# Keys turned by the DMA instead of by the matrix engine, with two small jobs moved between engines

## The reference, cut to what matters

```python
xn = _layernorm(x, ln1_w, ln1_b)               # x: the context, 16 x 1601 x 128
ln = _layernorm(latents, ln2_w, ln2_b)         # 16 x 64 x 128
q = ln @ Wq
kv = jnp.concatenate([xn, ln], axis=-2) @ Wkv
k, v = jnp.split(kv, 2, axis=-1)               # heads: 16 x 64
logits = jnp.einsum('bhld,bhsd->bhls', q * scale, k * scale)
w = jax.nn.softmax(logits, axis=-1)
out = jnp.einsum('bhls,bhsd->bhld', w, v)
return out.reshape(B, L, INNER) @ Wo
```

## Time and profile before

| | |
|---|---|
| median of 3 runs | 2209.73 us |
| the profiled execution | 2206.32 us, span 2204.6 us |
| PE busy | 2042.9 us (93%) |
| DVE busy | 1704.4 us (77%) |
| ACT busy | 1370.1 us (62%) |
| POOL busy | 566.5 us (26%) |
| first cross attention | from 7 us to 932 us |
| second cross attention | from 1168 us to 2041 us |
| DMA in all | 95.18 MB, mean 43 GB/s |

### The profile page before, as it was taken

One profiled execution on the slowest core, in us unless ns is written; L12 is line 12 of the kernel. 1 busy time (PEld: TensorE's weight loads), 2 busy tenths in 40 slices (PEclk: granted clock), 3 DMA queues, 4 the chain that ended last, 5 costly groups with the idle time before them and its releaser, 6 DMA issues. The chain is left out here.

```text
span 2204.6 us, 38627 instructions
## 1 busy us (share of the span) xinstructions
PE 2042.9 (93%) x11914; PEld 1118.3 (51%) x11914; DVE 1704.4 (77%) x4268; ACT 1370.1 (62%) x2468; POOL 566.5 (26%) x584
## 2 busy tenths in 40 slices
PE   7899999999999999889798999999999999999786
PEld 5454545454545455533566444454545454544584
DVE  7789797988888887589667777777786868685557
ACT  3377676766666676644323587868687878777211
POOL 4433333333333332059101102121111111110000
PEclk9899999999999999989999899999999999999897
DMA  2211111111010100033103011111111011100100
GB/s 80 78 48 48 48 48 47 47 47 54 40 63 31 63 31 32 9 93 124 47 1 109 5 36 55 52 35 36 35 36 35 36 35 36 35 32 1 28 1 10
DMA packets 40903, 95.18 MB, mean 43 GB/s; under 512 B 11436, under 2 KB 26776, under 8 KB 40760
## 3 DMA queue, kind: packets, MB, share of 16 engines
q1 hardware_dynamic: 40760, 93.61, 12.3%
HBM read 65.15 MB, written 27.92 MB: 42 GB/s over the span
## 5 line engine op out<-in xcount | busy, mean ns | idle before, releaser
L1122 DVE TENSOR_TENSOR x_p_lo<-x_psum,x_p_hi 128x512 f16<-128x512 f32 (+2 forms) x896 | 606.4, 683 | 195.4 <-ACT x_psum L913 159.5
L912 ACT ACTIVATE x_p_hi<-x_psum 128x512 f16<-128x512 f32 (+2 forms) x480 | 287.9, 600 | 267.8 <-PE x_psum L750 266.0
L912 ACT ACTIVATE x_p_hi<-x_psum,x_bcol 128x512 f16<-128x512 f32 (+1 forms) x416 | 292.3, 703 | 104.2 <-PE x_psum L750 102.3
L770 PE MATMUL x_psum<-x_p_hi,x_x_both 128*128 128x512 f16 (+1 forms) x832 | 316.8, 381 | 42.3 <-DVE x_p_lo L1122 42.1
L748 PE MATMUL x_psum<-x_q,x_xT_both 128*128 128x512 f16 x832 | 316.6, 381 | 0.2
L772 PE MATMUL x_psum<-x_p_hi,x_x_both 128*128 128x512 f16 (+1 forms) x832 | 315.8, 380 | 0.0
L771 PE MATMUL x_psum<-x_p_lo,x_x_both 128*128 128x512 f16 (+1 forms) x832 | 315.8, 380 | 0.0
L750 PE MATMUL x_psum<-x_q,x_xT_both 128*128 128x512 f16 x832 | 315.6, 379 | 0.0
L749 PE MATMUL x_psum<-x_q,x_xT_both 128*128 128x512 f16 x832 | 315.6, 379 | 0.0
L913 ACT ACTIVATE x_psum<-x_psum 128x512 f32<-128x512 f32 (+2 forms) x480 | 287.3, 598 | 0.6
L825 PE MATMUL x_psum<-x_xT_both,x_q 128*128 128x512 f16 (+2 forms) x1024 | 268.3, 340 | 18.4 <-DVE x_mx L1068 6.4
(11 more groups left out here) (450 smaller groups left out, 3404.6 us busy)
## 6 DMA issues: line engine op xcount, KB each, us to landing
context_rows<-x_x_both SPq DMA_DIRECT2D x16, 832.0 KB, 3.5
context_cols<-x_xT_both SPq DMA_DIRECT2D x16, 832.0 KB, 4.9
x_xT_both<-context_cols SPq DMA_DIRECT2D x16, 832.0 KB, 4.5
x_x_both<-context_rows SPq DMA_DIRECT2D x16, 832.0 KB, 6.3
x_raw<-in_ctx SPq DMA_DIRECT2D x16, 768.0 KB
ssm_c_row<-ssm_bc_rows SPq DMA_DIRECT2D x16, 512.0 KB, 4.3
ssm_b_wide<-ssm_bc_rows SPq DMA_DIRECT2D x7, 512.0 KB
x_mrow<-in_mask_BxS_bk SPq DMA_DIRECT2D x16, 200.1 KB
```

Of the source, the lines that this page charges most:

```text
L770: pe.matmul(out, v_hi, p_hi[r][rows, :], start=start, stop=False)
L912: act.activation(p_hi[r][rows, :], score[r][rows, :], ACT.Exp, scale=SCORE_UNIT, **bias).then_inc(p_hi_ready, 1)
L1122: v.tensor_tensor(p_lo[r][rows, :], score[r][rows, :], p_hi[r][rows, :], ALU.subtract).then_inc(p_lo_ready, 1)
```

## The change

In words:

- The first layer's `x` items are gone from PE, ACT and DVE. POOL splits `xt` right after it has normalized it, into a new buffer `x16` (`halves`). SP stores `x16` to `context_rows`, waits until the store has landed, and loads `xT_both` back from there by transposing DMAs in three parts: `front` (hi, tiles 0 to 6), `back` (hi, tiles 7 to 12) and `low` (lo, all 13 tiles), then `x_both` by a plain DMA.
- The second layer loads `xT_both` in the same three parts from `context_rows`; `context_cols` is gone.
- `max` items come in another order: the eight that need only `front` first, then the eight that need `back`. They begin in unit 2 of a first body (before: 4 in the first layer, 3 in the second) and in unit 6 of a second one.
- The latents' sums are copied by DVE instead of ACT, and `later_high` goes from ACT to POOL.
- Mean and variance of the 13 tiles come from five instructions on 13 columns instead of 13 bn_aggr.
- The mask's row and column forms are made at two different places. The last three pairs are handled as: loop of pairs 1 to 5, pairs 6 and 7 unrolled.
- In the folding part POOL normalizes and splits context 0, and SP stores it and issues its loads before the block ends.

```diff
-NORM_STEPS = 2 * KT + 1 + RSQRT_STEPS
+NORM_STEPS = KT + 5 + 1 + RSQRT_STEPS
...
+        def turned_part(sp, n, par, s, j, k):
+            rows = kept_rows[bass.ds(n, 1), :, s:s + 1, j:k, :].rearrange("o p s j d -> (o p) (s j d)")
+            out = xT_both[par][:, s, j * P:k * P].rearrange("p (j k) -> p j k", k=P)
+            return sp.dma_start(out, rows, transpose=True)
+        def load_xT_front(sp, n, par):
+            turned_part(sp, n, par, 0, 0, FRONT).then_inc(xT_front[par], 16)
+        def load_xT_rest(sp, n, par):
+            turned_part(sp, n, par, 0, FRONT, KT).then_inc(xT_back[par], 16)
+            turned_part(sp, n, par, 1, 0, KT).then_inc(xT_low[par], 16)
+        def store_x(sp, n):
+            wait_alone(sp, x16_ready, n + 1)
+            sp.dma_start(kept(n), x16[:, :, :, :]).then_inc(x_stored, 16)
+            wait_alone(sp, x_stored, 16 * (n + 1))
...
+        def halves(pool, n):
+            if not (isinstance(n, int) and n == 0):
+                wait_alone(pool, x_stored, 16 * n)
+            wait_alone(pool, xt_ready, n + 1)
+            pool.tensor_copy(x16[:, 0, :, :], xt[:, :, :]).then_inc(x_hi_ready, 1)
+            wait_alone(pool, x_hi_ready, n + 1)
+            pool.tensor_tensor(x16[:, 1, :, :], xt[:, :, :], x16[:, 0, :, :], ALU.subtract).then_inc(x16_ready, 1)
...
-                for j in range(KT):
-                    steps.mark(v.bn_aggr(xmv[:, j, :], xstats[:, j, :]))
+                (even, even_m2), (odd, odd_m2) = ((xstats[:, :, k + 1], xstats[:, :, k + 2]) for k in (0, 3))
+                steps.mark(v.tensor_tensor(xd[:, :], even, odd, ALU.subtract))
+                steps.mark(v.tensor_tensor(xm2[:, :], even_m2, odd_m2, ALU.add))
+                steps.wait()
+                steps.mark(v.scalar_tensor_tensor(xmean[:, :], xd[:, :], -0.5, even, ALU.mult, ALU.add))
+                steps.mark(v.scalar_tensor_tensor(xd2[:, :], xd[:, :], 0.25, xd[:, :], ALU.mult, ALU.mult))
+                steps.wait()
+                steps.mark(v.scalar_tensor_tensor(xvar[:, :], xm2[:, :], 1.0 / D, xd2[:, :], ALU.mult, ALU.add))
...
                         load_raw(sp, 1, 1, 0)
+                        store_x(sp, 0)
+                        load_xT_front(sp, 0, 0)
+                        load_xT_rest(sp, 0, 0)
+                        load_x(sp, 0, 0)
...
-    PAUSE = ((0, 1), (1, 0)) if masked else ((1, 1), (0, 0))
-    LEAD = (2, 0) if masked else (0, 0)
+    PAUSE = ((0, 1), (1, 0))
+    LEAD = (1, 0)
+    MAX_ORDER = [*range(0, 2 * NC_, 2), *range(1, 2 * NC_, 2)]
...
             def body(at):
+                if at.has_next2 and masked:
+                    wait_alone(sp, bcol_ready, at.b + 1)
+                    load_mask(at.b + 2, at.par)
+                if at.has_next:
+                    rows(at)
+                if at.has_next3 and not masked:
+                    sp.wait_ge(xt_ready, at.b + 2)
+                    load_raw(sp, at.b + 3, at.npar, at.ni + 1)
                 if at.has_next2:
...
+                    if not masked:
+                        store_x(sp, at.b + 2)
+                    wait_alone(sp, s_ready, at.half + 2 * FRONT)
+                    sp.wait_ge(held["prep_done"], 1)
+                    load_xT_front(sp, at.b + 2, at.par)
+                    wait_alone(sp, s_ready, at.half + 2 * KT)
+                    sp.wait_ge(held["prep_done"], 1)
+                    load_xT_rest(sp, at.b + 2, at.par)
+                    wait_alone(sp, pv_done, at.half + 2 * KT)
+                    sp.wait_ge(held["prep_done"], 1)
+                    load_x(sp, at.b + 2, at.par)
...
                 if kind == "max":
                     if a == 0:
...
+                        pe.wait_ge(hi_ready, at.n * HI_PARTS + (HI_PARTS if at.npar == 0 else 4))
+                        pe.wait_ge(xT_front[at.npar], (at.ni + 1) * 16)
+                    if a == 1:
+                        pe.wait_ge(xT_back[at.npar], (at.ni + 1) * 16)
...
             def body(at):
-                if at.par == 0 and not masked:
-                    later_low(at, 0)
                 if at.has_next:
...
+                        mask_col(at.n, at.npar, at.ni, None if at.first and at.par == 0 else at.half - 2)
+                    if at.par == 0:
+                        later_high(at)
+                        later_low(at)
+                if at.par == 0 and not at.first:
+                    wait_alone(pool, pv_done, at.half)
+                    pair(at.i)
...
+                        context_normal(pool, wait_alone, at.b + 2, at.par)
+                        halves(pool, at.b + 2)
...
+                    if u == 1 and not (at.first and at.par == 0):
+                        latents_sums(at.half, 1 - at.par)
```

More of the change, by code:

```diff
@@ L564, in attention_loop, with __init__ @@
     class At:
-        def __init__(self, i, par, first, last):
+        def __init__(self, i, par, first, last, near):
             self.i, self.par, self.first, self.last = i, par, first, last
@@ L575, in __init__ @@
             self.has_next2 = not last
+            self.has_next3 = not last and not (near and par == 1)
         def place(self, item):
@@ L699, in before @@
                 if not masked:
[L700 to L724 removed]
+                    sp.wait_ge(xt_ready, 1)
```

236 lines of the change are left out of this document (92 added, 144 removed).

## The result

The changed kernel has a median of 2177.36 us (2174.71 to 2183.13, 4 runs), the kernel before one of 2209.32 us beside it. The ratio is 0.9857 (95% interval 0.9835 to 0.9879), 32 us faster. Four more runs, later, gave 2177.61 us (0.9876, 0.986 to 0.9893). The forecast of 2197 us had the direction, and the range 2172 to 2230 holds the time, but the gain is more than twice the 12.5 us foretold. It came out at the number of rival 3 (2176), not for rival 3's reason.

What follows compares the result with a forecast made beforehand. PE was taken as near its limit everywhere, DVE's chain as setting first-layer first bodies. -14 - 5 + 8.5 - 2 = -12.5 took 2206.3 to 2193.8; the median's 3.4 more gave 2197 us, range 2172 to 2230.

Steps and rivals of the forecast that it cites:

- rival 3: PE sets all bodies: first-layer first bodies fall by 26 us instead of 5, total -33, so 2176 us; chance 0.12.
- the two stretches counted as nothing: Between the two layers' attention marks and behind the last mark: forecast 0 us each.
- Second bodies, -14: First layer: seven second bodies fall from 51.77 to 49.8 us each as PE work and waits go; bounds -11 and -16.
- First bodies, -5: First layer: eight first bodies, set by DVE's chain, gain 0.7 us each; bounds 0 and -26.
- VectorE's sum was to be -3.3: First-layer first bodies: DVE's removed and added work and stretching together shorten its chain by 3.3 us a body.
- a stretching that goes: First-layer first bodies: small DVE steps lengthened beside POOL's subtraction return to normal, about 1.0 us a body in all.
- the +2.6 of the two units behind the maxima: First-layer first bodies: two units move behind the maxima, PE needing 1.3 us for each, +2.6 us.
- The second layer, -2: Second-layer first bodies gain 0.3 us each from ACT's lost jobs and earlier maxima; bounds +4 and -8.
- The front: First transposing load lands 4 us after issue, 10.5 us behind the body's end, in time for unit 2 at no cost.
- rival 1: Late front: its load takes 8 us, 3.5 us late in eight first bodies, +28 us, so 2225 us; chance 0.20.
- The start: Store and loads before the block boundary delay PE from 40.6 to 51; net +8.5 us, bounds +7 and +15.
- What was to come back ahead of it, 2.1 us: At the start, before the first shift: DVE no longer makes the lo half, regaining 2.08 us.

Runs made afterwards that it cites:

- Run 11: Changed kernel with 13 f32 transposes put back on PE in a lump ahead of the first maximum of every first-layer body; 2206.19 us (0.9987).
- Run 12: Changed kernel with 13 f32 transposes put back on PE, one ahead of each of the first 13 maxima of a first-layer body; 2193.55 us (0.9956).
- run 3: Changed kernel with VectorE's sum of the two constant rows (L1081) made behind the fifth maximum instead of the last but two; 2175.01 us (0.9851).
- run 2: Changed kernel with the old places and order of the maxima in both layers; 2216.96 us (1.0043).
- Run 1: Changed kernel with the later context's query copies (later_high) and the latents' sums copy both back on ScalarE; 2187.95 us (0.9912).
- run 13: Changed kernel with later_high and the latents' sums copy back on ScalarE and, in the second layer alone, the old maxima places and order; 2191.6 us (0.9937).
- run 4: Changed kernel with the store of the context's two halves issued ahead of SyncE's wait for the shift; 2176.47 us (0.9862).
- run 14: Changed kernel profiled again without an edit; between the layers 360.58 us instead of 354.86, second layer 739.7 instead of 740.0.
- runs 8 and 9: First: changed kernel with only the latents' sums copy back on ScalarE, 2211.6 us. Second: that kernel with ScalarE's second-layer loop written out, 2182.45 us.

## Why the prediction was right and where it failed

The kernel gained 17.9 us more than the forecast's 12.5, by the first of the two profiles. The second layer has 11.5 of it, the second bodies 4.9, the two stretches counted as nothing 5.4, the start 0.9; first bodies took 4.8 back. So two misses of opposite sign hide in a total that lies at rival 3's number by luck.

**Second bodies, -14, measured -18.9: mis-sized.** The step took the second layer's 49.46 as a floor and a value above it. PE's own rows had most of the answer: 1.48 us of transposes and two waits of 0.60 and 0.63 us at the change from `x` to `max`. That they add up to 2.71 where each body fell by 2.70 is in part chance, since the changed kernel has a new wait of 0.51 us there; by the windows PE's busy time fell by 1.83 us (50.14 to 48.31) and its idle time by 0.87 (1.63 to 0.76). Run 11 gives the transposes by themselves, 1.42. The other layer was no floor: PE is idle there for 49.46 - 48.35 = 1.11 us, more than the 0.76 here.

**First bodies, -5, measured -0.2 and -2.4: the mechanism right, a term wrong.** Run 12 shows that 13 more matmuls of PE don't lengthen them, and run 3 that 1.4 us taken out of VectorE's chain shorten them by 1.1 to 1.3. In the kernel before, the five in the loop all end 51.53 or 51.54 us behind their first `p_lo`, though this starts between 4.33 and 4.69 us into the body. The last of the seven has no statistics and fell by 2.2 us; the other six stand at +1.9 and -0.3 together, where the forecast had six times -0.7. VectorE's sum was to be -3.3 and is -2.1. The five instructions take 0.76 us (0.75 foretold), the copy 1.2. What failed is "a stretching that goes": 1.4 us of it came back at L1081, shown by run 3. With the +2.6 of the two units behind the maxima, which is measured at 17.0 against 14.4 us, the balance in the loop is +0.5. The body of pair 6, in the loop before and outside it now, has no late start and went from 56.23 to 54.69. The Trainium skill has the rule for this stretching ("SBUF — State Buffer", SBUF: two separate sides): VectorE and GpSimd take a pair of SBUF ports exclusively, for a whole instruction; a VectorE operation with two SBUF inputs takes part in this against a GpSimd operation that reads SBUF. The trace agrees for GpSimd's subtraction: in the changed kernel and in run 2 the sum ends 0.27 and 0.26 us behind it, whenever it began, and operations with an input from PSUM beside it keep their 0.67 us. It doesn't for GpSimd's normalizing, which reads SBUF too: beside it, in run 3, the sum takes 0.41 us.

**The second layer, -2, measured -13.5: the step that failed.** The forecast reasoned that PE is idle for only 2.1 us in a first body, "so little can come of it", and gave 0.3 of it. That was true as a bound and wrong as a size: 1.3 us of it in the mean were taken in each of seven bodies by the two moves. What filled them was not one wait but a late row: ScalarE's exponential of unit 2 at +5.1, then every `p_lo` behind it, then the first maximum. Run 1 (0.7 a body), run 2 (0.7) and run 13 (both, 1.2 to 1.6) show it. The rest, 0.65 us a loop body, is a shorter stall behind the branch: VectorE's first `p_lo` is at +3.4 instead of +4.1 to +5.2, and in the kernel before all five loop bodies end 48.47 us behind it. Nobody designed that. The bound itself was too low for these bodies, since the one that was read, 52.83, was among the shortest: the five took 52.6 to 53.7.

**The front: right.** 3.7 us to landing against 4 assumed; 10.6 us behind the body's end against 10.5 borne. In the loop it costs at most 0.3 us of VectorE; in the body of pair 1, which has no late start, PE waits 1.48 and 0.68 us for it (run 4). Run 2 shows how near rival 1 was: the second load, wanted in the next item, is 2.8 us late. By the Trainium skill's 1309 ns a block ("VectorE: DVE Perf Modes", The three transpose paths) the seven blocks would take 9.2 us; the whole trip took 3.9. The 261 GB/s of the Trainium skill ("DMA: Bandwidth & Descriptors", Latency and other measured facts), with the 2 us taken from the earlier trace rows, gave an estimate of 2.9 and stood nearer.

**The start: the number right, by luck.** +7.6 and +9.5 against 8.5, but from other parts. PE went on at 53.6, later than the 51 foretold: GpSimd's and SyncE's chain is as computed up to 48.4, but the three transposing issues hold the queue 4.2 us. The half clock, which the forecast named only for its bound, made it worse: VectorE's steps behind the first queries come every 1.28 us until 59.6, and every 0.67 us once the clock is back, as they did before from the first on. So the first shift came at 86.1 and not near 80. What was to come back ahead of it, 2.1 us, did not; 6.6 us came back behind it, 4.5 of them by VectorE's shorter wait for the raw context, which the forecast had seen and counted as nothing.

**Not foreseen:** 5 us between the marks and at the end, the first of them scatter by run 14. That at the end (-2.5 and -2.6) lies within the 173.2 to 177.4 us that this stretch took over all kernels; its cause stays open.

## What to carry to other kernels

Sum the waits of the engine that is nearly full, item by item, before you compare with another stage; and when its slack is small, ask which late row upstream fills that slack in every pass, since a small bound times many bodies is still a gain. When an operation beside another engine's stops being stretched, look for the next instruction that the moved work will lie beside. Do not put transfers ahead of a boundary that every engine waits for when their first user is far behind it.

## What the runs showed of the hardware

- **What a backward branch costs differs from program to program.** VectorE's first `p_lo` comes 1.9 to 2.4 us later behind one than without in the first layer of the changed kernel; in the second layer 0.8 to 1.0 us later, and 1.7 to 2.8 in the kernel before. ScalarE loses nothing in the changed kernel, and 5.8 to 6.3 us in one whose only edit was a copy moved to it: 29 us in all (runs 8 and 9). What decides it no run shows. A stall with the reason "issue" at the head of a loop body, or with a releaser that was long done, is therefore to be read before an edit is judged.
- **Transposing loads are cheap here.** 26 blocks of 128x128 f16 in three loads need 4.2 to 4.3 us of the issuing queue, and a load lands 3.7 us behind its issue (median of 96).
- **The same code scatters.** The stretch between the layers took 354.9 and 360.6 us in two executions of the same kernel, and 354.9 to 361.0 in all 18 profiled ones (some edits touch its last body), while second bodies of the changed kernel, 49.07 us, repeat within 0.02 us. Gains of a few us are better read from bodies than from a median.
